# Fourteen pairs of fields instead of twelve, two of their sums on VectorE, other first loads, and dense rows on four row groups

## The chip, the cores and the metric

The kernel runs on one core of one Trainium2 chip. The metric is the device time of one execution in microseconds (us), lower is better. Its engines are PE (TensorE, matrix products), DVE (VectorE), ACT (ScalarE), POOL (GpSimd) and SP (SyncE, which here only issues DMAs). All data are float32.

## What is computed

```python
# e: 512 samples x 39 fields x 16 numbers, one table row per sample and field
e = stack([tbl_f[ids[:, f]] for f in range(39)], axis=1)
x, prev, logit = e, e, []
for k in range(3):                       # three "cross" layers, 128 units each
    z = einsum('bmd,bhd->bdmh', x, prev).reshape(b, D, m * h)
    t = transpose(einsum('bdc,co->bdo', z, ws[k]) + bs[k], (0, 2, 1))
    t = t / sqrt(sum(t * t, axis=(-2, -1), keepdims=True))
    logit.append(t); prev = t
z = sum(concatenate(logit, axis=1), axis=-1)            # 512 x 384
h = maximum(concatenate([z, dense_ctx], axis=1) @ W_top1 + b_top1, 0)   # dense_ctx: 512 x 16
h = maximum(h @ W_top2 + b_top2, 0)
y = h @ W_top3
```

## The kernel before

**Tiles.** The 512 samples go in 16 tiles of 32. A tile's columns are sample and embedding index, N = 32 x 16 = 512, split in two halves N1 and N2 of 256. POOL gathers the table rows by ten indirect DMAs for each tile (`gather`), SP writes them to DRAM as `xt` (one row of 512 numbers for each field) and reads them back spread over partitions.

**Layers 1 and 2** are called k = 1 and k = 2; both have 128 x 39 products in each column. DVE multiplies the previous layer's output (in the PSUM bank `t_ps`) by one field's row on all partitions (`xb`) and writes the product to a ring `z` of 14 slots; PE multiplies `z` by that field's 128 x 128 weights. The 39 fields go in 11 chunks for each layer; "chunk (k, c)" below is chunk c of layer k. `PLAIN_IN` writes the order out: a number n is a plain chunk of n fields (`direct`, two matmuls of 512 columns for each field, one for the left and one for the right 64 weight columns), a 0 is a pair chunk (`pairs`): four fields as two pairs, each pair by a scheme of seven block products instead of eight, so 14 matmuls of 256 columns for a pair chunk. A pair chunk needs sums of its products, which POOL makes (`pair_sums`): first t2 (128 x 512), then t4 and t1 together (128 x 1024, "t41" here). PE starts a pair chunk with eight matmuls on `z` alone, then two on t2, then four on t41. `sums` has two slots, so POOL can be at most two pair chunks ahead of PE; `RING_AT` places chunks in the ring, so that DVE can be two or three ahead.

**Between layers**, `carry` (ACT) and `shared_sums`, `add_shared` (DVE) put the shared parts of the pair scheme together once the last pair chunk is done, and PE may not begin the next layer's first pair chunk before that. PE does layer 0 of the next tile (`layer0`, 14 matmuls of 512 columns) between layer 1 and layer 2 of a tile; DVE prepares it (`products0`) with `xr`, 19 shifted copies of the fields, times `x3`, which ACT first copies to PSUM (`copy_x`). Every engine works through its own list in the written order; semaphores order them.

**Gathers.** POOL issues the ten gathers of tile i + 2 during tile i: five behind the last pair chunk (1, 9) of layer 1, five behind (2, 9). `mix_rows` (POOL) makes combined rows for the pairs behind the first pair chunk.

**The start** gathers tile 0, writes it, loads `xr` and `x3` for tile 0, then all `xb` chunks, then the weights w2, then the rows of tile 1; ACT's list for tile 0 begins with `copy_x(1)`. **The end** is three dense layers; the first has four output blocks of 128, each from three blocks of features and, by a matmul of its own (L794), the 16 dense inputs.

Of the kernel before, what the change touches and what calls it, by code (L numbers as in the profile page):

```python
# [50 lines left out]
PAIR_GROUPS = 3  # L51
PAIRED = 2 * GROUP * PAIR_GROUPS
PAIRS = PAIRED // 2
PLAIN_IN = [3, 3, 0, 0, 3, 0, 0, 3, 0, 0, 3]


def chunks():

    out, field, p = [], PAIRED, 0
    for n in PLAIN_IN:  # L60
        out.append(("D", field, n) if n else ("P", p, 4))
        field, p = field + n, p + (not n)
    return out
# [32 lines left out]


def pair_fields(p):  # L100

    q, j = p // 2, 2 * (p % 2)
    return [(2 * GROUP * q + j + r, 2 * GROUP * q + GROUP + j + r) for r in range(2)]


def build(nc, ids_in, base_in, masks_in, table, xt, xq, dense_t, w0a, w0b, w1, w2, b0, b1, b2,
          wt1, bt1, wt2, bt2, wt3, out):
    ctx = ExitStack()
# [755 lines left out]
```

## Time and profile before

| | |
|---|---|
| Median of the runs shown | 1181.57 us |
| Lowest of them | 1180.67 us |
| The profiled execution's own time | 1181.07 us |
| Its span, first to last instruction | 1179.2 us |
| PE busy | 1124.8 us, 95% |
| DVE busy | 972.1 us, 82% |
| POOL busy | 868.3 us, 74% |
| ACT busy | 126.4 us, 11% |

One of the three runs took 4874.38 us; the median leaves it aside. The profile gives each engine's busy time over the span of one execution. Each float32 matmul of the program is two instructions in it. A busy share near 100% says that an engine is the bound only where no other row shows it waiting, so the trace is read tile by tile.

### The profile page before, as it was taken

The page shows a single profiled execution, that of the slowest core. Times are in us where ns is not written, and L with a number is a line of the kernel's source. Part 1 is how long each engine was busy: PE and PEld are TensorE (multiplying, and loading weights), DVE is VectorE, ACT ScalarE, POOL GpSimd, SP SyncE. Part 2 cuts the span into 40 slices and gives each one's busy share as a digit, 9 for nine tenths or more (in the row PEclk, how much of TensorE's full clock was granted, in tenths as well). Part 3 has the DMA queues.
Part 4 walks back from the last instruction along what each step waited for, and adds up shares of the span by engine and source line. Part 5 has one row for each costly group of instructions (what it writes and reads, how often), then busy time and mean ns, then how long its engine had stood idle before and what let it go on. Part 6 is the DMA issues. An engine that isn't in the chain of part 4 may idle for free. (4 is left out here: it accounts for less than half of the span.)

```text
span 1179.2 us, 21810 instructions
## 1 busy us (share of the span) xinstructions
PE 1124.8 (95%) x7868; PEld 568.1 (48%) x7868; DVE 972.1 (82%) x836; ACT 126.4 (11%) x266; POOL 868.3 (74%) x614
## 2 busy tenths in 40 slices
PE   0789999999999999999999999999999999999999
PEld 0344445455444545544454554545455454545553
DVE  1678889889898988988898898989889898988782
ACT  0000110101011010101101011110101011010102
POOL 5567768788786878877686886868788786856670
PEclk9889999999999999999999999999999999999999
DMA  5958446382744638274463837546382845637010
GB/s 163 382 150 277 142 165 211 98 294 68 286 131 162 210 96 299 68 280 136 144 220 97 306 68 263 154 167 208 95 296 68 282 134 176 211 104 274 1 47 1
DMA packets 104409, 204.31 MB, mean 173 GB/s; under 512 B 49131, under 2 KB 52075, under 8 KB 104390
## 3 DMA queue, kind: packets, MB, share of 16 engines
q1 hardware_dynamic: 97610, 202.52, 51.9%
q0 software_dynamic: 5120, 1.29, 1.1%
q10 hardware_dynamic: 1660, 0.25, 0.2%
q8 instruction: 12, 0.20, 0.1%
q14 instruction: 7, 0.06, 0.0%
HBM read 201.72 MB, written 2.30 MB: 173 GB/s over the span
## 5 line engine op out<-in xcount | busy, mean ns | idle before, releaser
L560 DVE TENSOR_TENSOR z<-t_ps,xb 128x2048 f32<-128x2048 f32 (+1 forms) x352 | 708.1, 2042 | 97.6 <-PE acc L711 73.8
L281 POOL TENSOR_TENSOR sums<-z,sums 128x1024 f32<-128x1024 f32 x192 | 455.4, 2372 | 15.1
L697 PE MATMUL acc<-z,w_sb 128*64 128x512 f32 x1920 | 436.5, 598 | 12.5 <-DVE z L560 12.5
L278 POOL TENSOR_TENSOR sums<-z 128x512 f32<-128x512 f32 x192 | 245.2, 1277 | 193.0 <-DVE z L560 189.2
L711 PE MATMUL mix_ps<-sums,s_sb 128*64 128x256 f32 x1536 | 282.6, 380 | 6.0 <-POOL sums L281 6.0
L697 PEld LDWEIGHTS acc<-z,w_sb 128*64 128x64 f32 x1920 | 137.8, 138 | 246.8 <-issue 224.8
L711 PE MATMUL acc<-z,w_sb 128*64 128x256 f32 x768 | 228.4, 379 | 0.0
L711 PE MATMUL mix_ps<-z,w_sb 128*64 128x256 f32 x768 | 228.4, 379 | 0.0
L711 PE MATMUL acc<-z,s_sb 128*64 128x256 f32 x768 | 228.4, 379 | 0.0
L711 PE MATMUL p_ps<-z,w_sb 128*64 128x256 f32 x768 | 228.4, 379 | 0.0
L711 PEld LDWEIGHTS mix_ps<-sums,s_sb 128*64 128x64 f32 x1536 | 158.8, 137 | 93.6 <-POOL sums L281 13.1
L243 POOL DMA_INDIRECT gathered<-in_table,rows_of x160 | 155.4, 971 | 64.2 <-issue 49.2
L711 PE MATMUL acc<-sums,w_sb 128*64 128x256 f32 x768 | 198.0, 380 | 0.0
L711 PEld LDWEIGHTS acc<-z,w_sb 128*64 128x64 f32 x768 | 105.3, 137 | 97.1 <-issue 55.5
L711 PEld LDWEIGHTS acc<-z,s_sb 128*64 128x64 f32 x768 | 105.2, 137 | 55.4
L688 PE MATMUL acc<-xr,w_sb 117*64 117x512 f32 (+1 forms) x448 | 100.7, 601 | 30.9 <-issue 30.9
L711 PEld LDWEIGHTS mix_ps<-z,w_sb 128*64 128x64 f32 x768 | 105.3, 137 | 0.0
L711 PEld LDWEIGHTS p_ps<-z,w_sb 128*64 128x64 f32 x768 | 105.2, 137 | 0.0
L711 PEld LDWEIGHTS acc<-sums,w_sb 128*64 128x64 f32 x768 | 103.6, 137 | 0.0
L688 PEld LDWEIGHTS acc<-xr,w_sb 117*64 117x64 f32 (+1 forms) x448 | 32.6, 139 | 95.6 <-issue 95.0
L543 DVE TENSOR_TENSOR xr<-t_ps,xr 117x1024 f32<-117x1024 f32 (+1 forms) x60 | 62.3, 1079 | 0.0
L448 ACT COPY cross<-mix_ps 64x256 f32<-64x256 f32 x32 | 11.6, 364 | 376.7 <-PE acc L711 351.1
(76 smaller groups left out, 404.9 us busy)
## 6 DMA issues: line engine op xcount, KB each, us to landing
xb<-xt SPq DMA_DIRECT2D x80, 768.0 KB, 6.8
xb<-xq SPq DMA_DIRECT2D x96, 512.0 KB, 4.7
xb<-xt SPq DMA_DIRECT2D x96, 512.0 KB, 6.3
xr<-xt SPq DMA_DIRECT2D x144, 156.0 KB
x<-xt SPq DMA_DIRECT2D x45, 78.0 KB
gathered<-in_table,rows_of POOLq DMA_INDIRECT x160
xr<-xt SPq DMA_DIRECT2D x32, 78.0 KB
xt<-gathered SPq DMA_DIRECT2D x16, 72.0 KB, 2.3
```

Of the source, the lines that this page charges most:

```text
L243: nc.gpsimd.indirect_dma_start(gathered[0:n, g, :], None, table[:, :], bass.IndirectOffsetOnAxis(rows_of[0:n, g:g + 1], 0)).then_inc(rows_ ...
L278: nc.gpsimd.tensor_tensor(t2, t3, b11, ALU.add).then_inc(sums_ready, 1)
L281: nc.gpsimd.tensor_tensor(t41, b2, t2_twice, ALU.subtract).then_inc(sums_ready, 1)
L448: nc.scalar.copy(cross[RIGHT, N2], mix_ps[LEFT, N2]).then_inc(cross_ready, 1)
L543: nc.vector.tensor_tensor(xr[0:n, k0:k1, :], x[0:n, :].rearrange("p (a n) -> p a n", a=1).broadcast_to([n, k1 - k0, N]), xr[0:n, k0:k1, :] ...
L560: nc.vector.tensor_tensor(z[:, at:at + n, :], t_ps[k - 1][:, :].rearrange("p (a n) -> p a n", a=1).broadcast_to([P, n, N]), xb[:, XB_ROW[c ...
L688: last = nc.tensor.matmul(acc0[o, :], w0_sb[0:n, k, o], xr[0:n, k, :], start=(k == 0), stop=(k == STEPS0 - 1))
L697: last = nc.tensor.matmul(acc[k][o, :], w_sb[k][:, field + r, o], z[:, at + r, :], start=(c == 0 and r == 0), stop=(c == NCH - 1 and r == ...
L711: return nc.tensor.matmul(bank[side, cols], weights, moving, start=start, stop=stop, skip_group_check=True)
```

## The change

- `PAIRS` goes from 12 to 14: seven pair chunks for each layer instead of six, eleven plain fields instead of fifteen, and `PLAIN_IN` is [2, 0, 3, 0, 0, 0, 0, 3, 0, 0, 3] with another `RING_AT`.
- For chunks (1, 5) and (1, 9) t2 is made by DVE (`later_t2`) right behind the chunk's product, from a copy of one operand that ACT makes in PSUM (`copy_b11`, behind `copy_x` in ACT's list). POOL makes the other twelve t2 of a tile and all fourteen t41.
- The gathers are split eight and two instead of five and five; the last gather has its own semaphore, and rows are written before it has landed.
- Layer 0's shifts are grouped so that one DMA on 117 partitions loads what three on 39 did (`load_shifted`, `load_x`); for tile 0, ACT's queue issues some of them. The masks are smaller and loaded apart from the ids.
- DVE's small steps are at other chunks; the mixing of the w2 weights in tile 0 is spread over four chunks; for tile 0 and the last tile the sum of squares comes first.
- The 16 dense inputs are loaded four times, at partitions 0, 32, 64 and 96, and the four matmuls for them each use one such group of 32 rows, one behind the other.

```diff
-PAIR_GROUPS = 3
-PAIRED = 2 * GROUP * PAIR_GROUPS
-PAIRS = PAIRED // 2
-PLAIN_IN = [3, 3, 0, 0, 3, 0, 0, 3, 0, 0, 3]
+PAIRS = 14
+PAIR_GROUPS = -(-PAIRS // GROUP)
+PLAIN_IN = [2, 0, 3, 0, 0, 0, 0, 3, 0, 0, 3]
...
+T2_LATER = {(1, 5): 0, (1, 9): 0}
...
-RING_AT = [0, 3, 6, 10, 0, 3, 7, 11, 0, 4, 8, 11, 0, 3, 7, 11, 0, 4, 8, 0, 4, 10]
+RING_AT = [0, 2, 6, 9, 0, 4, 8, 0, 3, 7, 0, 0, 2, 6, 9, 0, 4, 8, 0, 3, 7, 11]
...
-                pool.wait_ge(rows_gathered, 16 * GROUPS * (i + 1))
-                if not at_first(i):
+                pool.wait_ge(rows_gathered, 16 * (GROUPS - 1) * (i + 1))
...
-                            gather(i + 2, range(0, 5))
+                            gather(i + 2, range(0, 8))
                         if k == 2 and c == LAST_P and gathers:
-                            gather(i + 2, range(5, GROUPS))
-                        if k == 2 and c == FIRST_P + 1 and last:
+                            gather(i + 2, range(8, GROUPS))
+                        if k == 2 and c == PADS_AT and last:
...
+            load_x(act, 0)
+            load_shifted(act, 0, 1)
+            load_shifted(act, 0, 3)
...
+            def copy_b11(i, k):
+                for c in range(NCH):
+                    if (k, c) in T2_LATER:
+                        act.wait_ge(z_ready, chunks_to(i, k, c))
...
+                        nc.scalar.copy(b11_ps[k].rearrange("p (r n) -> p r n", r=2), z[:, at:at + 2, N1]
+                                       ).then_inc(b11_copied, 1)
...
                     copy_x(i + 1)
+                copy_b11(i, 1)
                 carry(i, 1)
...
+            def later_t2(i, k, c):
...
+                        wait_slot(dve, i, k, cc)
+                        dve.wait_ge(b11_copied, t2_count(i, k, cc))
+                        nc.vector.tensor_tensor(sums[:, slot, 0, :, :], z[:, at:at + 2, N2],
+                                                b11_ps[k].rearrange("p (r n) -> p r n", r=2),
+                                                ALU.add).then_inc(vector_t2, 1)
...
                     products(i, 1, c)
-                    if c == 2 and not first:
+                    later_t2(i, 1, c)
+                    if c == 1 and not first:
                         shared_sums(i - 1, 2)
-                    if c == 5 and not first:
+                    if c == 3 and not first:
                         add_shared(i - 1, 2)
-                    if c == 6 and not first:
+                    if c == 7 and not first:
                         norm_sums(2, i - 1)
-                    if c == 6 and first:
-                        mixed_weights(2)
+                    if c >= NCH - 4 and first:
+                        mixed_weights(2, c - NCH + 4)
...
-                    if c == 10:
+                    if c == 8:
                         normalize(i + 1, *layers_of(first, last))
...
-                nc.tensor.matmul(h1_ps[j][:, :], wt1d_sb[:, o], dense_sb[:, :], start=False, stop=False)
+
+            for j in range(TOP1 // P):
+                r = slice(j * DENSE_AT, (j + 1) * DENSE_AT)
+                nc.tensor.matmul(h1_ps[j][:, :], wt1d_sb[r, :], dense_sb[r, :], start=False, stop=False)
```

How it moves instructions, at three places. **POOL, where a tile of the loop goes from layer 1 to layer 2**, before: the two sums of chunk (1, 9), five gathers, the sums of the first pair chunk of layer 2.

```order
L278 TENSOR_TENSOR sums<-z 128x512 [waits z_used,z_ready]
L279 ISA
L281 TENSOR_TENSOR sums<-z,sums 128x1024 [waits sums_ready]
L235 REGISTER_ALU
L237 ISA [waits mixed_ready,xt_written]
L237 TENSOR_TENSOR rows_of<-ids_sb,base_sb 128x10
L239 REGISTER_ALU
L243 DMA gathered<-in_table,rows_of 128x16 [waits rows_ready]
L243 DMA gathered<-in_table,rows_of 128x16 x4
L269 REGISTER_ALU
L278 TENSOR_TENSOR sums<-z 128x512 [waits z_used,z_ready]
```

The same place in the changed kernel (the line numbers are its own):

```order
L335 REGISTER_ALU [waits z_used]
L341 TENSOR_TENSOR sums<-z,sums 128x1024 [waits vector_t2]
L293 REGISTER_ALU
L295 ISA [waits mixed_ready,xt_written]
L295 TENSOR_TENSOR rows_of<-ids_sb,base_sb 128x10
L297 REGISTER_ALU
L301 DMA gathered<-in_table,rows_of 128x16 [waits rows_ready]
L301 DMA gathered<-in_table,rows_of 128x16 x7
L337 REGISTER_ALU [waits z_used]
L338 TENSOR_TENSOR sums<-z 128x512 [waits z_ready]
```

POOL now waits for DVE's t2 at (1, 9), and eight gathers instead of five stand ahead of layer 2's first sums.

**ACT in tile 0**, before: the evacuation of layer 0, a root, the copy of x3 for tile 1, and then the steps behind layer 1.

```order
L431 ACTIVATE sq<-acc,bias 128x512 [waits acc0_ready]
L432 ACTIVATE traw<-acc,bias 128x512
L473 ACTIVATE nrm_ps<-nrm_ps 128x32 [waits nrm_ready]
L439 COPY t_ps<-x 117x512 [waits z_ready,x3_loaded]
L448 COPY cross<-mix_ps 64x256 [waits z_used]
```

And in the changed kernel:

```order
L492 ACTIVATE sq<-acc,bias 128x512 [waits acc0_ready]
L493 ACTIVATE traw<-acc,bias 128x512
L550 ACTIVATE nrm_ps<-nrm_ps 128x32 [waits nrm_ready]
L504 COPY t_ps<-x 117x512 [waits feat_ready,x3_loaded]
L515 COPY acc<-z 128x512 [waits z_ready]
L515 COPY acc<-z 128x512 [waits vector_t2,z_ready]
L525 COPY cross<-mix_ps 64x256 [waits z_used]
```

The two copies for DVE's sums stand behind the copy of x3 for tile 1, which waits for that load.

**DVE in tile 0**, in the changed kernel, from the product of chunk (1, 2) on:

```order
L643 TENSOR_TENSOR z<-t_ps,xb 128x1536
L643 TENSOR_TENSOR z<-t_ps,xb 128x2048 x3
L656 TENSOR_TENSOR sums<-z,acc 128x512
L643 TENSOR_TENSOR z<-t_ps,xb 128x2048
L643 TENSOR_TENSOR z<-t_ps,xb 128x1536
L612 TENSOR_TENSOR s_sb<-w_sb 128x768
L612 TENSOR_TENSOR s_sb<-w_sb 128x128
```

The first sum L656 stands between the products of chunks (1, 5) and (1, 6); before, the products of the two chunks followed each other.

## Rows read from the trace of the kernel before

**Rows 1.** The page: busy us (share of the span) and instructions by engine.
```profile
PE 1124.8 (95%) x7868; PEld 568.1 (48%) x7868; DVE 972.1 (82%) x836; ACT 126.4 (11%) x266; POOL 868.3 (74%) x614
```

**Rows 2.** Windows of two whole tiles: us, busy us (instructions) by engine, PEclk, DMA, GB/s.
```profile
226.11:294.37 68.26, 68.26 (x490) 34.57 (x488) 60.06 (x52) 7.54 (x16) 53.84 (x39) 1.00 0.55 180
294.37:364.52 70.15, 68.63 (x490) 34.74 (x488) 60.15 (x52) 7.53 (x16) 53.98 (x39) 1.00 0.53 175
```

**Rows 3.** Timeline of PE in the first of them: start, us, what.
```profile
226.11 6.18 PE L688 MATMUL acc<-xr,w_sb 117*64 117x512 f32 x28
232.12 5.32 PE L697 MATMUL acc<-z,w_sb 128*64 128x512 f32 x24
...
239.00 0.81 PE L711 MATMUL mix_ps<-sums,s_sb 128*64 128x256 f32 x5
...
242.02 0.81 PE L711 MATMUL mix_ps<-sums,s_sb 128*64 128x256 f32 x5
...
247.62 0.81 PE L711 MATMUL mix_ps<-sums,s_sb 128*64 128x256 f32 x5
```

**Rows 4.** Groups by line and shape: count, busy us, mean ns, idle before.
```profile
L281 POOL TENSOR_TENSOR sums<-z,sums 128x1024 f32<-128x1024 f32 x192 | 455.4, 2372 | 15.1
L560 DVE TENSOR_TENSOR z<-t_ps,xb 128x2048 f32<-128x2048 f32 x192 | 437.5, 2286 | 74.1 <-PE acc L711 73.8
...
L278 POOL TENSOR_TENSOR sums<-z 128x512 f32<-128x512 f32 x192 | 245.2, 1277 | 193.0 <-DVE z L560 189.2 <-issue 3.7
...
L243 POOL DMA_INDIRECT gathered<-in_table,rows_of x160 | 155.4, 971 | 64.2 <-issue 49.2 <-POOL rows_of L237 13.1
...
L591 DVE TENSOR_TENSOR acc<-acc,v 128x512 f32<-128x512 f32 x16 | 11.0, 690 | 0.1
```

**Rows 5.** Timelines at one change of layer: POOL's last sum, ACT's first copy.
```profile
565.43 2.37 POOL L281 TENSOR_TENSOR sums<-z,sums 128x1024 f32<-128x1024 f32 x1
```
```profile
569.79 0.36 ACT L448 COPY cross<-mix_ps 64x256 f32<-64x256 f32 x1 [16.28 <-PE acc L711]
```

**Rows 6.** Timelines: two gathers with a gap, and a wait of PE.
```profile
332.04 0.94 POOL L243 DMA_INDIRECT gathered<-in_table,rows_of  x1 [2.49 <-issue]
```
```profile
343.80 0.43 PE L711 MATMUL mix_ps<-sums,s_sb 128*64 128x256 f32 x1 [1.28 <-POOL sums L281]
```
```profile
917.10 0.94 POOL L243 DMA_INDIRECT gathered<-in_table,rows_of  x1 [2.24 <-issue]
```

**Rows 7.** Timelines of the start: SP, DVE and PE.
```profile
23.59 3.84 SPq L343 DMA_DIRECT2D xr<-xt  x9
```
```profile
34.78 1.82 DVE L543 TENSOR_TENSOR xr<-x,xr 117x1024 f32<-117x1024 f32 x2 [1.79 <-DMA xr<-xt]
```
```profile
30.92 8.01 PE L688 MATMUL acc<-xr,w_sb 117*64 117x512 f32 x28 [30.92 <-issue]
```

**Rows 8.** Windows of the start, in the columns of Rows 2.
```profile
30.00:32.50 2.50, 1.58 (x4) 0.59 (x6) 1.51 (x2) 0.00 (x0) 2.20 (x2) 1.00 1.07 209
...
35.00:40.00 5.00, 3.93 (x20) 1.08 (x16) 1.60 (x2) 1.03 (x2) 3.38 (x4) 1.00 1.02 409
```

**Rows 9.** Timelines of tile 0: SP, ACT, PE, and PE's start of tile 1's layer 0.
```profile
69.73 1.16 SPq L338 DMA_DIRECT2D x<-xt  x3
```
```profile
72.62 0.59 ACT L439 COPY t_ps<-x 117x512 f32<-117x512 f32 x1 [30.29 <-DMA x<-xt]
```
```profile
73.76 5.34 PE L697 MATMUL acc<-z,w_sb 128*64 128x512 f32 x12 [4.84 <-DVE z L560]
...
87.55 6.18 PE L688 MATMUL acc<-xr,w_sb 117*64 117x512 f32 x28
```

**Rows 10.** Timeline of PE in the last tile and behind it.
```profile
1121.73 5.37 PE L697 MATMUL acc<-z,w_sb 128*64 128x512 f32 x24 [3.53 <-DVE z L560]
...
1155.74 1.02 PE L794 MATMUL acc<-xb 128*128 128x512 f32 x2
1156.60 1.88 PE L792 MATMUL acc<-feat,xb 128*128 128x512 f32 x4
```

More of the change, by code:

```diff
@@ L32, with pair_fields @@
 STEPS0 = -(-SHIFTS // PER_STEP)
-SHIFT_OF = [[PER_STEP * k + j + 1 for j in range(PER_STEP)] for k in range(STEPS0 - 1)] + [[SHIFTS - 1, 0]]
+SHIFT_OF = [[k + STEPS0 * j for j in range(PER_STEP) if k + STEPS0 * j < SHIFTS] for k in range(STEPS0)]
 WIDE = PER_STEP * FIELDS
-NARROW = 2 * FIELDS
+NARROW = len(SHIFT_OF[-1]) * FIELDS
 XT_ROWS = FIELDS + SHIFTS - 1
 LOADS0 = [(0, 2), (2, 4), (4, 6), (6, 7)]
-PAIR_GROUPS = 3
-PAIRED = 2 * GROUP * PAIR_GROUPS
-PAIRS = PAIRED // 2
-PLAIN_IN = [3, 3, 0, 0, 3, 0, 0, 3, 0, 0, 3]
+PAIRS = 14
+PAIR_GROUPS = -(-PAIRS // GROUP)
+PLAIN_IN = [2, 0, 3, 0, 0, 0, 0, 3, 0, 0, 3]
+def pair_fields(p):
+    q, j = p // 2, 2 * (p % 2)
+    return [(2 * GROUP * q + j + r, 2 * GROUP * q + GROUP + j + r) for r in range(2)]
 def chunks():
-    out, field, p = [], PAIRED, 0
+    out, p = [], 0
+    paired = [m for p in range(PAIRS // 2) for ab in pair_fields(p) for m in ab]
+    plain = [m for m in range(FIELDS) if m not in paired]
     for n in PLAIN_IN:
-        out.append(("D", field, n) if n else ("P", p, 4))
-        field, p = field + n, p + (not n)
+        out.append(("D", plain[0], n) if n else ("P", p, 4))
+        plain, p = plain[n:], p + (not n)
     return out
@@ L68, with chunk_of @@
 XB_ROW = [sum(n for _, _, n in CHUNKS[:c]) for c in range(NCH + 1)]
+def chunk_of(row):
+    return next(c for c in range(NCH) if XB_ROW[c + 1] > row)
+PADS_AT = next(c for c in range(chunk_of(4), NCH) if CHUNKS[c][0] == "P")
 FIRST_P = PLAIN_IN.index(0)
@@ L72 @@
 STEPS = 2 * NCH
+PAIR_CHUNKS = [(k, c) for k in (1, 2) for c in range(NCH) if CHUNKS[c][0] == "P"]
+T2_LATER = {(1, 5): 0, (1, 9): 0}
+VECTOR_T2 = [kc for kc in PAIR_CHUNKS if kc in T2_LATER]
+POOL_T2 = [kc for kc in PAIR_CHUNKS if kc not in T2_LATER]
 RING = 14
-RING_AT = [0, 3, 6, 10, 0, 3, 7, 11, 0, 4, 8, 11, 0, 3, 7, 11, 0, 4, 8, 0, 4, 10]
+RING_AT = [0, 2, 6, 9, 0, 4, 8, 0, 3, 7, 0, 0, 2, 6, 9, 0, 4, 8, 0, 3, 7, 11]
 def ring_back(s):
@@ L90 @@
 SUM_SLOTS = 2
+QUADS = [q for q in ((0, PAIRS // GROUP, GROUP), (PAIRS // GROUP, 1, PAIRS % GROUP)) if q[2]]
 LEFT, RIGHT = slice(0, UNITS // 2), slice(UNITS // 2, UNITS)
@@ L97 @@
 DENSE = 16
-def pair_fields(p):
-    q, j = p // 2, 2 * (p % 2)
-    return [(2 * GROUP * q + j + r, 2 * GROUP * q + GROUP + j + r) for r in range(2)]
+DENSE_AT = 32
 def build(nc, ids_in, base_in, masks_in, table, xt, xq, dense_t, w0a, w0b, w1, w2, b0, b1, b2,
@@ L121, in build @@
         rows_of = sb("rows_of", [P, GROUPS], I32)
-        masks = sb("masks", [P, 2, PAIR_GROUPS, EMB])
+        masks = sb("masks", [P, 2])
         gathered = sb("gathered", [P, GROUPS, EMB])
@@ L657, in _ @@
             dve.wait_ge(w0b_loaded, 16)
[L659 to L663 removed]
+            nc.vector.tensor_tensor(w0_sb[:, :, :], w0_sb[:, :, :], w0m, ALU.add).then_inc(w0_ready, 1)
+            for part in range(4):
+                mixed_weights(1, part)
             products0(0, range(len(LOADS0)))
[L665 to L666 removed]
+            sum_squares(0, 0)
+            sum_d(0, 0, dsum_alone)
+            normalize(0, 0, 1, dsum_alone)
             scale0(0)
@@ L765, in tile @@
                     layer0(i + 1)
-                layer(i, 2, range(0, 7), first)
+                layer(i, 2, range(0, 6), first)
                 add_partitions(i + 1, *layers_of(first, last))
-                layer(i, 2, range(7, NCH), first)
-            pe.wait_ge(w0_ready, 2)
+                layer(i, 2, range(6, NCH), first)
+            pe.wait_ge(w0_ready, 1)
             pe.wait_ge(ones_ready, 1)
```

226 lines of the change are left out of this document (134 added, 92 removed).

## The prediction

> **What bounds the kernel now.** I read the page's busy shares first, then single tiles. PE is busy for 95% of the span, DVE for 82%, POOL for 74% [rows 1]. The windows of two whole tiles say how firm that is: in one of 68.26 us PE is busy for all 68.26, while DVE has 60.1 and POOL 53.8 of busy time [rows 2]. So in a plain tile PE is the bound and nothing waits. The next window is 70.15 us long, and 1.5 us of it is PE idle: POOL was late. The engine behind PE is POOL, though its busy share hides that: its gathers cost more than their busy time. The group has 971 ns for each of 160 gathers and 49.2 us of "issue" before them [rows 4], so about 1.25 us each with the usual gap of 0.3. A tile costs POOL 12 x (1.28 + 2.37) + 10 x 1.25 + some 2 for row numbers and mixing, that is 58 of 68 us. And buffers are short: `sums` holds two pair chunks, so POOL's spare time can't be saved up.
>
> PE's prices come from its timeline [rows 3]: the same point of two pair chunks in a row is 3.02 us apart (239.00 and 242.02); the next is 5.60 later, with three plain fields between, so a plain field is 2.58 / 3 = 0.86; layer 0 is 6.01 (226.11 to 232.12).
>
> **1. The extra pair chunk.** In each layer four plain fields (3.44) become a pair chunk (3.02): -0.42. Of 32 layers, the first is counted in step 3; 31 x 0.42 = **-13.0 us**. This lies on PE, the bound, and it is real only where PE stays fed.
>
> **2. Feeding PE in a plain tile.** POOL now has 14 x 2.37 + 12 x 1.28 + 12.5 + 2 = 63 us of 67.4: two t41 more. DVE gets two 128x512 sums at 0.69 [rows 4], each behind an ACT copy of about 0.6, so 60.1 + 1.4 busy and 1.3 of waiting: 63 too. Neither is over PE's 67.4, so the question is the places where work meets. I walked the new order with these durations; the tight place is the change from layer 1 to 2. Let PE end chunk (1, 5) at 0. DVE's product (1, 8) is there at 2.4, one part of `xr` at 3.5, product (1, 9) at 5.7; ACT's copy ends at 6.5, DVE's t2 at 7.3, POOL's t41 at 9.7. PE needs it 2.2 into (1, 9), at 10.8: 1.1 to spare, near the lead that POOL has now (its sum ends at 567.80, PE's chunk at about 569.7, its last four matmuls take 0.9) [rows 5]. Then POOL does row numbers and eight gathers: 0.2 + 0.8 + 1.0 + 7 x 1.25 = 10.8, to 20.5; then t2 and t41 of (2, 1), to 24.2. PE meanwhile: end of (1, 9) 11.6, of (1, 10) 14.2, of layer 0 20.2, two fields to 22.0, and t41 wanted at 24.1. Before, POOL had 6.8 us of gathers and PE six fields instead of two between the same points: 3.4 + 4 less room now. So the spare time is zero, 0.1 short. The run of four pair chunks (2, 3) to (2, 6) also eats 0.65 of lead for each chunk (3.67 on POOL against 3.02); at (2, 6) the two meet within 0.1, at (2, 9), behind DVE's scaling steps that moved to c = 8, POOL is 0.1 late. Sum of the walk 0.2 us a tile, 14 tiles of the loop: **+2.8 us**. Bounds: 0, where my walk is 0.3 pessimistic at each place, and 1.0 a tile, 14 us, where it is 0.3 optimistic at each of three places. I take the walk itself. The new early wait of PE at FIRST_P = 1 for the shared sums costs nothing: ACT's and DVE's steps take some 3.3 us (an estimate: two copies and five small sums) from the end of (2, 9), PE has 2.6 + 1.7 of work.
>
> **3. Start and tile 0.** ACT's copy for DVE's t2 of (1, 5) stands behind `copy_x(1)`, and that waited for its load until 72.62 [rows 9]. Before, nobody needed it early; PE had a wait of 4.84 there anyway, for w2 at DVE. Now DVE, and everything behind it on DVE's list (products (1, 6) on, the w2 weights), stands still until the load lands, with PE stopped inside (1, 5), which it would reach near 56 to 58. When does it land? The loads start about 2.0 earlier than 23.59 [rows 7] (masks apart, rows written before the last gather). The first loads move slowly, 209 GB/s with the DMA engines full, against 409 later [rows 8]; they are 2 KB pieces on 39 partitions and become 4 KB pieces on 117. At the later rate that would give up to 4 more; I take 1.8. So the load lands near 68.8, ACT's two copies end at 70.1, DVE's t2 at 70.8. From there, at 0: POOL t41 2.4, PE ends (1, 5) 3.2; DVE (1, 6) 2.2, POOL 6.1, PE ends (1, 6) 7.0 and (1, 7) 9.6, (1, 8) 12.6; DVE (1, 9) 11.9 after the weights' first parts, t2 13.3, POOL 15.7, PE ends (1, 9) 16.6; DVE's (1, 10) 17.4, PE 20.0. PE's layer 0 of tile 1 starts at 90.8 instead of 87.55: **+3.2 us**, though the very first matmuls come some 5 us earlier. The bounds are the load's: 66.6 to 72.6, that is +1 to +7. PE's clock is at half behind the stop (twelve instructions took 5.34 at 73.76 [rows 9], three fields take 2.58 elsewhere [rows 3]), but there PE waits for POOL most of the time; I leave it in the range. One short wait more at tile 0's (2, 1), where DVE is late as well: **+0.6**.
>
> **4. The gathers' gaps.** At about every 29th gather of the run POOL stops: 2.49 us at 332.04, 2.24 at 917.10, two others like them [rows 6]. A gap in the second batch cost PE its length less 0.6 (70.15 - 68.26 = 1.9 for 2.49 [rows 2]; one of its two waits is in [rows 6]); the one at 917.10 fell in the first batch, where the room was wide, and cost nothing. With eight gathers in the first batch the 58th, 87th and 145th all fall there, and there is no room now: 2 x 0.6 + 2.2 = **+3.4 us**. Bounds 0 and +8 (a fourth gap).
>
> **5. The last tile's change of layer**, without a layer 0 as cover. PE waited 3.53 [rows 10]. The first product is shorter by 0.5, but behind it PE has two fields instead of six: it waits 0.5 for the product of (2, 1), then 1.6 for t41, and 0.9 in the run of four: 6.0 instead of 4.0, **+2.1 us**.
>
> **6. The dense rows.** Four matmuls of 0.86 (1155.74 to 1156.60) at the end, on the path. Two instructions each, so 0.43 for one [rows 10]. No row shows row groups. The nearest are the left and right column halves: there 24 instructions of the same 512 columns take 5.3, 0.22 each [rows 3], so two halves overlap fully. I take it that four on four row groups take one's time: **-2.6 us**, bound 0. The matmuls left between the norm's one and its use are five, 4.3 us, more than the chain of small operations beside them (some 2, an estimate from their short forms).
> The Trainium skill ("TensorEngine Tiling (Array Packing)", Key Properties) has two rules here that pull apart: tiles "can execute LdWeights and Matmul in parallel", and changing the tiling mode "drains the TensorE". By the first the sum stays as it is; by the second alone the gain is smaller. No row here tells the price of a drain.
>
> **Sum.** -13.0 + 2.8 + 3.2 + 0.6 + 3.4 + 2.1 - 2.6 = -3.5. The span of 1179.2 becomes 1175.7; the profiled execution's own time is 1.9 above its span, and the median 0.5 above that: **1178 us**.
>
> **Rivals.**
> A. *PE stays fed.* Steps 2 and 4 cost nothing and the load of step 3 lands early: -13.0 - 2.6 + 1.0 + 2.1 = -12.5, 1169 us; with tile 0 better by 4 still, 1165. For it: POOL and DVE are below PE in every total. Against: totals of 63 against 67 with two slots of buffer. Chance 0.27.
> B. *POOL becomes the bound*, slower than before. Place: eight gathers ahead of (2, 1). If a gather costs 0.1 more in a batch of eight (at the start, in batches of ten, several took longer), or DVE's t2 comes 1 us later, PE waits 1 us in each tile, and each gap counts in full: -3.5 + 11 + 4 = +11.5, 1193 us. It beats the gain from about 0.45 us a tile on. Chance 0.2.
> C. *The row groups do not overlap:* the -2.6 is gone, 1181 us. The skill's rule on mode changes would do this. Chance 0.08, as the column halves speak for overlap.
>
> **How the numbers follow.** My forecast, 1178, has 0.45. The range of 8 in 10 runs from the middle of A to B: 1164 to 1192. A measurement of this kernel tells about 2% from no change; faster by that means under 1158, which needs all of A and 7 us more: 0.04. Slower by it, over 1205, needs B at twice its price: 0.02. Within 2%: 0.94.
>
> **What would show it.** Plain tiles: layer 0 to layer 0 near 67.6; PE waits on POOL's sums in (2, 1) up to 0.4, and of 2 to 3 us in about three tiles, with a gap among the eight gathers. Tile 0: ACT's copy of x3 ends near 69.5, DVE's first L656 right behind, PE stopped over 10 us before it. PE's layer 0 of tile 1 starts near 91. The four dense matmuls within 1 us. I am wrong if waits of PE are in other places (the shared sums, DVE's products), or if the load for tile 1 comes before 60.

## The result, and the profile after

The changed kernel takes **1254.43 us** (median of four runs, 1252.67 to 1258.84) against 1181.12 for the kernel before on the same chip: a ratio of 1.063 with a 95% interval of 1.059 to 1.067. It is slower by 6%, where I had forecast 1178 us and a range up to 1192. The span of the profiled execution is 1257.0 us, against 1179.2.

The page of the changed kernel, busy time by engine (before: [rows 1]):
```profile
PE 1131.8 (90%) x8252; PEld 589.7 (47%) x8252; DVE 995.2 (79%) x875; ACT 144.3 (11%) x298; POOL 946.6 (75%) x646
```
PE has only 7 us more of busy time, so 71 of the 78 us more of span are waiting. Where, is told by PE's starts of layer 0, in tile 1 and in tile 15 (timeline of PE in the changed kernel):
```profile
127.62 5.66 PE L798 MATMUL acc<-xr,w_sb 117*64 117x512 f32 x24
...
1125.36 6.18 PE L798 MATMUL acc<-xr,w_sb 117*64 117x512 f32 x28
```
Before, tile 1's came at 87.55 [rows 9] and tile 15's at 1049.85 (timeline of PE in the kernel before):
```profile
1049.85 6.18 PE L688 MATMUL acc<-xr,w_sb 117*64 117x512 f32 x28
```
So the start and tile 0 lose 40.1 us, the 14 tiles between lose 997.7 - 962.3 = 35.4 (71.3 us a tile), and the rest 2.3. Both losses have one name, in the view of waits of the changed kernel (waited for: us in total, times, longest):
```profile
ACT t_ps L504 <- DMA x<-xt: 79.6, 15, 29.1
DVE xr L626 <- DMA xr<-xt: 75.3, 30, 12.8
...
PE acc L798 <- DVE xr L626: 55.6, 3, 41.7
...
PE mix_ps L821 <- POOL sums L341: 26.0, 23, 2.1
PE acc L807 <- DVE z L643: 25.7, 17, 3.7
```
ACT and DVE wait for the loads of x3 and `xr`. PE itself never waits for a DMA, it waits for POOL's sums and DVE's products, which stand behind those two on their engines' lists. In a plain tile (SP, ACT and DVE timelines of the changed kernel, 671 to 700):
```profile
671.55 0.79 SPq L272 DMA_DIRECT2D x<-xt  x1
672.45 10.28 SPq L279 DMA_DIRECT2D xr<-xt  x4
...
677.65 0.59 ACT L504 COPY t_ps<-x 117x512 f32<-117x512 f32 x1 [3.26 <-DMA x<-xt]
...
678.79 0.69 DVE L656 TENSOR_TENSOR sums<-z,acc 128x512 f32<-128x512 f32 x1 [1.37 <-ACT acc L515]
...
696.19 1.22 DVE L626 TENSOR_TENSOR xr<-t_ps,xr 117x1024 f32<-117x1024 f32 x1 [1.92 <-DMA xr<-xt]
699.40 0.69 DVE L626 TENSOR_TENSOR xr<-t_ps,xr 78x512 f32<-78x512 f32 x1 [1.99 <-DMA xr<-xt]
```
x3 is issued at 671.55 and is there at 677.65; the last part of `xr` lands at 699.40, 28 us behind the first issue. How the DMA engines spend that time is in the windows of the changed kernel (last columns: PEclk, DMA share, GB/s):
```profile
672.00:677.50 5.50, 5.50 (x43) 2.79 (x40) 5.38 (x4) 1.34 (x2) 5.34 (x4) 1.00 0.19 55
...
683.00:690.00 7.00, 7.00 (x56) 3.79 (x54) 7.00 (x6) 0.00 (x0) 5.67 (x4) 1.00 0.19 77
```
and in a window of the kernel before, over the loads of the same data:
```profile
552.00:556.00 4.00, 4.00 (x28) 1.85 (x26) 3.58 (x4) 1.48 (x3) 3.92 (x3) 1.00 0.81 216
```
The share of the 16 DMA engines stands at 0.19, which is 3 of 16, for 25 us; before it is 0.81, which is 13 of 16. The merged source counts 3 shifts in its outermost dimension and 39 fields in the next; before, each DMA's outermost dimension counted 39, and 13 is its largest divisor up to 16.

The Trainium skill ("DMA: Bandwidth & Descriptors", section "Why a DMA increments its semaphore by 16 and not by 1", at "How many engines (k)") states this: the slowest dimension of size over 1 of source and destination decides, and the largest k up to 16 that divides both is the number of engines. By it 3 and 117 give 3, 39 and 39 give 13; the trace agrees with 0.19 and 0.81. I had not drawn on it. The same page of the Trainium skill ("Rules for kernel authors") also has that "an outermost dim of size c < 16 [...] confines the whole DMA to at most c engines".

Tile 0 pays first for its own loads. Timelines of PE and ACT at the start of the changed kernel, where PE stops inside layer 0 each time until the next part of `xr` has landed and been multiplied by DVE:
```profile
41.69 3.68 PE L798 MATMUL acc<-xr,w_sb 117*64 117x512 f32 x8 [41.69 <-DVE xr L626]
55.59 5.83 PE L798 MATMUL acc<-xr,w_sb 117*64 117x512 f32 x16 [10.21 <-DVE xr L626]
65.10 1.97 PE L798 MATMUL acc<-xr,w_sb 78*64 78x512 f32 x4 [3.67 <-DVE xr L626]
...
67.12 0.69 ACT L492 ACTIVATE sq<-acc,bias 128x512 f32<-128x512 f32 x1 [63.45 <-PE acc L798]
```
Before, PE did this layer in one go from 30.92 on, 8.01 us long [rows 7]; so 28 us are lost before layer 1 of tile 0 begins. The wait for tile 1's x3 is then no longer than before: ACT waits 29.07 us for it, where it waited 30.29, until 72.62 [rows 9]. It only comes later, and DVE now stands behind it (SP, ACT and DVE in the changed kernel):
```profile
91.92 0.76 SPq L272 DMA_DIRECT2D x<-xt  x1
...
98.30 0.59 ACT L504 COPY t_ps<-x 117x512 f32<-117x512 f32 x1 [29.07 <-DMA x<-xt]
98.83 0.58 ACT L515 COPY acc<-z 128x512 f32<-128x512 f32 x1
...
99.51 0.69 DVE L656 TENSOR_TENSOR sums<-z,acc 128x512 f32<-128x512 f32 x1 [14.73 <-ACT acc L515]
```
A whole tile of the changed kernel in one window, to be held against [rows 2]:
```profile
626.64:697.91 71.27, 68.32 (x515) 36.20 (x513) 61.06 (x53) 8.65 (x18) 58.98 (x41) 1.00 0.52 173
```
PE is idle for 3 us in each tile, two waits of over 1 us, for DVE's product and for POOL's sum (PE's timeline of the changed kernel):
```profile
634.08 1.94 PE L807 MATMUL acc<-z,w_sb 128*64 128x512 f32 x8 [1.26 <-DVE z L643]
...
640.08 0.43 PE L821 MATMUL mix_ps<-sums,s_sb 128*64 128x256 f32 x1 [1.42 <-POOL sums L341]
```
Two things are better than before. The longest gap ahead of a gather is 0.3 us, where [rows 6] have 2.49 and 2.24 (waits of POOL in the changed kernel):
```profile
POOL gathered L301 <- issue: 40.3, 135, 0.3
```
And the four dense rows run beside each other: those in the last rows of PE's timeline start within 0.55 us, where before each took 0.86 [rows 10], 3.4 for the four:
```profile
1241.38 0.70 PE L906 MATMUL acc<-xb 32*128 32x512 f32 x2
...
1241.91 0.59 PE L906 MATMUL acc<-xb 32*128 32x512 f32 x2
```

### The profile page after: what moved, and what is told of

Same layout as the page of the kernel before. It is cut to its first block and busy times, and to the rows that moved or that the text cites. A ratio compares the mean times of both kernels' runs of the same rounds, so it can differ in the third digit from the quotient of the medians.

```text
span 1257.0 us, 22412 instructions
## 1 busy us (share of the span) xinstructions
PE 1131.8 (90%) x8252; PEld 589.7 (47%) x8252; DVE 995.2 (79%) x875; ACT 144.3 (11%) x298; POOL 946.6 (75%) x646
## 5 line engine op out<-in xcount | busy, mean ns | idle before, releaser
L643 DVE TENSOR_TENSOR z<-t_ps,xb 128x2048 f32<-128x2048 f32 (+2 forms) x352 | 705.1, 2040 | 49.4 <-PE acc L821 37.3
L341 POOL TENSOR_TENSOR sums<-z,sums 128x1024 f32<-128x1024 f32 x224 | 533.0, 2380 | 56.2 <-DVE sums L656 41.2
L821 PE MATMUL mix_ps<-sums,s_sb 128*64 128x256 f32 x1792 | 338.5, 382 | 36.5 <-POOL sums L341 26.0
L807 PE MATMUL acc<-z,w_sb 128*64 128x512 f32 x1408 | 328.2, 603 | 25.7 <-DVE z L643 25.7
L821 PE MATMUL acc<-z,w_sb 128*64 128x256 f32 x896 | 268.7, 382 | 3.6 <-DVE z L643 3.6
L821 PE MATMUL mix_ps<-z,w_sb 128*64 128x256 f32 x896 | 268.6, 382 | 0.0
L821 PE MATMUL acc<-z,s_sb 128*64 128x256 f32 x896 | 267.4, 380 | 0.0
L821 PE MATMUL p_ps<-z,w_sb 128*64 128x256 f32 x896 | 267.4, 380 | 0.0
L821 PEld LDWEIGHTS mix_ps<-sums,s_sb 128*64 128x64 f32 x1792 | 182.3, 137 | 150.7 <-POOL sums L341 52.0
L821 PE MATMUL acc<-sums,w_sb 128*64 128x256 f32 x896 | 233.8, 383 | 0.0
L656 DVE TENSOR_TENSOR sums<-z,acc 128x512 f32<-128x512 f32 x32 | 22.0, 688 | 51.2 <-ACT acc L515 50.5
```

Source lines behind the costliest of these rows:

```text
L341: nc.gpsimd.tensor_tensor(t41, b2, t2_twice, ALU.subtract).then_inc(t41_ready, 1)
L643: nc.vector.tensor_tensor(z[:, at:at + n, :], t_ps[k - 1][:, :].rearrange("p (a n) -> p a n", a=1).broadcast_to([P, n, N]), xb[:, XB_ROW[c ...
L656: nc.vector.tensor_tensor(sums[:, slot, 0, :, :], z[:, at:at + 2, N2], b11_ps[k].rearrange("p (r n) -> p r n", r=2), ALU.add).then_inc(vec ...
L807: last = nc.tensor.matmul(acc[k][o, :], w_sb[k][:, field + r, o], z[:, at + r, :], start=(c == 0 and r == 0), stop=(c == NCH - 1 and r == ...
L821: return nc.tensor.matmul(bank[side, cols], weights, moving, start=start, stop=stop, skip_group_check=True)
```

## The experiments

Theory 1: the merged loads' outermost dimension confines them to 3 engines, and x3 and `xr` land late; all else is near my forecast. Rivals: 2, the rest of the change costs it (pairs, gathers, PE badly fed); 3, ACT's list alone, where the copies for DVE's sums stand behind x3's. "Split" below means loads on 39 partitions. Ratios are to the kernel before, in runs on the same chip.

**1. Split loads in the changed kernel.**
```diff
-            src = bass.AP(blk.tensor, blk.offset, [[0, PER_STEP], [N, FIELDS], [1, N]])
-            engine.dma_start(x3[:, :], src).then_inc(x3_loaded, 16)
+            for j in range(PER_STEP):
+                engine.dma_start(x3[j * FIELDS:(j + 1) * FIELDS, :], blk[0:FIELDS, :]).then_inc(x3_loaded, 16)
```
and the same for `xr`, one DMA for each shift.

> The changed kernel with each merged load of x3 and xr taken apart again: three DMAs (two for the last step) on 39 partitions each, with the new shifts and 4 KB pieces. Nothing else differs. Theory 1 (the merged loads run on 3 of the 16 DMA engines, because their outermost dimension is 3: the DMA share was 0.19 = 3/16 while they ran alone): they get the speed of before, tile 0 loses its 28 us of late loads, the plain tiles their waits behind layer 0 (71.3 to about 67.7 us a tile), and the time falls to 1178 us, the sum of the prediction, 1165 to 1192. Theory 2 (the seventh pair chunk, the sums on VectorE and the new order are themselves too tight, the late loads only a symptom): the time stays over 1230 us.

Measured: 1182.9 us, ratio 1.0005 (0.9994 to 1.0017), span 1181.0. 76 of the 78 us are gone: 24.1 up to layer 0 of tile 1, 48.1 in the 14 tiles, 3.8 behind them. A tile takes (1053.13 - 103.54) / 14 = 67.83 us, and in one PE is idle for 0.08 (window of the kernel with split loads):
```profile
578.20:646.00 67.80, 67.72 (x514) 36.44 (x512) 60.93 (x54) 8.72 (x18) 58.76 (x40) 1.00 0.56 181
```
Theory 1 holds, rival 2 falls as the cause of the 6%. Tile 0 stays bad: layer 0 of tile 1 starts at 103.54, 16 us later than before. Timelines of SP, ACT, DVE and POOL there, in the same kernel:
```profile
46.88 22.87 SPq L383 DMA_DIRECT2D xt<-gathered  x4
...
71.72 1.15 SPq L272 DMA_DIRECT2D x<-xt  x3
...
74.49 0.59 ACT L505 COPY t_ps<-x 117x512 f32<-117x512 f32 x1 [31.09 <-DMA x<-xt]
...
75.70 0.69 DVE L657 TENSOR_TENSOR sums<-z,acc 128x512 f32<-128x512 f32 x1 [16.35 <-ACT acc L516]
...
80.17 3.30 DVE L613 TENSOR_TENSOR s_sb<-w_sb 128x768 f32<-128x768 f32 x2
...
80.20 3.12 POOL L342 TENSOR_TENSOR sums<-z,sums 128x1024 f32<-128x1024 f32 x1
```
DVE stands still for 16.35 us behind ACT's copy, which waits for x3 as I had written, but x3 lands at 74.5 and not at 68.8. Its load is issued no earlier than before (71.72 against 69.73 [rows 9]): SP is busy for 22.87 us issuing the four writes of tile 1's rows that stand ahead of it, so the earlier start did not reach this load.

**2. The kernel before with merged loads**, nothing else changed (its shifts are grouped as in the change).

> The kernel before with the merged loads alone (shifts k, k + 7, k + 14 in one DMA on 117 partitions; x3 in one DMA; tile 0 as well, on the queues of before). Theory 1: tile 0's layer 0 is late by some 25 to 30 us, and tile by tile the last part of xr lands 20 to 22 us after the first is issued, some 3 us after DVE wants it: 1220 to 1250 us. Theory 2: within 1% of the kernel before, 1170 to 1193.

Measured: 1304.58 us, ratio 1.102 (1.099 to 1.105). The merged loads alone cost 10% in the old kernel, more than in the new and more than either theory's number; the cause is the same (its view of waits):
```profile
DVE xr L540 <- DMA xr<-xt: 105.0, 46, 9.8
PE acc L691 <- DVE z L557: 71.1, 18, 4.6
```
One part of the higher cost is that PE runs slower here. Page, PE's timeline in one tile, and the window behind the stop, in this kernel:
```profile
PE 1167.8 (90%) x7868; PEld 571.8 (44%) x7868; DVE 977.4 (75%) x835; ACT 126.5 (10%) x266; POOL 865.2 (66%) x614
```
```profile
650.73 8.24 PE L691 MATMUL acc<-z,w_sb 128*64 128x512 f32 x24 [4.00 <-DVE z L557]
```
```profile
650.00:656.00 6.00, 5.28 (x14) 1.58 (x16) 6.00 (x4) 0.64 (x2) 1.31 (x2) 0.50 0.69 253
```
PE stops for 4.00 us in one piece, and behind it the granted clock is 0.50 of full speed; the 24 matmul instructions take 8.24 us instead of 5.32 [rows 3]. So 43 of the 124 us of added span are PE busy for longer over the same 7868 instructions (1167.8 against 1124.8 [rows 1]). In the changed kernel the stops in a tile are 1.26 and 1.42, and its clock over the tile is 1.00. Why the stop is longer in the old kernel was not tested; its rows are written behind five gathers of the second batch instead of two, so the same slow load starts later.

**3 and 4. The two t2 of DVE back on POOL**, with merged and with split loads.
```diff
-T2_LATER = {(1, 5): 0, (1, 9): 0}
+T2_LATER = {}
```

> The changed kernel with all fourteen t2 on GpSimd and no copies in PSUM, merged loads kept. Theory 1: xr still lands late, so the time stays within 15 us of the changed kernel, 1240 to 1270 us. Theory 3 (the late load of x3 acts only through ACT's list, where the copy for VectorE's sum stands behind it): tile 0 and the plain tiles recover most of the loss, under 1215.

> Both edits: loads taken apart and all t2 on GpSimd. Beside e1_split it prices the two sums on VectorE. If GpSimd is as near its limit as the prediction had it (63 of 67.4 us a tile), 2.6 us more a tile make it wait-bound: 10 to 20 us slower than e1_split in the plain tiles, less some 8 us in tile 0, where nothing stands behind x3's copy: 0 to +12 us in all. If VectorE's list is the tight one, it is faster than e1_split by 5 us or more.

Measured: merged 1251.57 us, ratio 1.058 (1.056 to 1.060), a tile still 71.5; split 1180.93, ratio 0.9992 (0.998 to 1.0003). Rival 3 falls as the whole cause: without any copy behind x3's the loss is nearly whole, through DVE's products of layer 0. (That ACT's list can carry a part of it is shown by experiment 10.) The split pair shows what DVE's sums are worth: with them on POOL a tile takes 68.58 us, 0.75 more, but layer 0 of tile 1 starts at 90.04, 13.5 us sooner. Gain in the loop and loss in tile 0 nearly cancel.

**5. ACT's copy for chunk (1, 5) ahead of x3's copy, in tile 0 only**, split loads.
```diff
+                if first:
+                    copy_b11(i, 1, range(0, 7))
                 if not last:
                     copy_x(i + 1)
-                copy_b11(i, 1)
+                copy_b11(i, 1, range(7 if first else 0, NCH))
```

> e1_split with one step moved in tile 0: ACT's copy for the sum of chunk (1, 5) ahead of its copy of x3 for tile 1. Theory: in e1_split PE stood 11.7 us in tile 0 for that sum alone. With it gone, tile 1's layer 0 starts near 90 us, as in e4_split_poolt2 (90.0), instead of 103.5, while the plain tiles keep 67.85: 1169 us. Rival: VectorE runs into the w2 weights and the x3 of tile 1 right behind, and gives most of it back: over 1177.

Measured: 1173.41 us, ratio 0.993 (0.991 to 0.995); layer 0 of tile 1 starts at 92.50 instead of 103.54. So 11 of the 16 us lost in tile 0 were that one place in ACT's list. The gain is less than the 2% at which I count a kernel as changed, but its interval lies below 1, as do those of experiments 9, 11 and 13.

**6. Tile 1's rows, x3 and `xr` ahead of the weights w2 on SP**, on top of 5.
```diff
-            sp.dma_start(w_sb[2][:, :, :], w2.rearrange("(m h) o -> h m o", h=P)).then_inc(w_loaded[2], 16)
             write_rows(1)
...
             load_layer0(1)
+            sp.dma_start(w_sb[2][:, :, :], w2.rearrange("(m h) o -> h m o", h=P)).then_inc(w_loaded[2], 16)
```

> e5_b11_first with SP's order in tile 0 changed: the rows, x3 and xr of tile 1 ahead of the load of w2, which needs less in front of it than they do. Expected: x3 for tile 1 is there some 8 us sooner, w2 some 8 later, in time for the mixing of its weights only if that does not stand in the way of the products: 1161 to 1171 us. Rival: VectorE, which mixes the w2 weights from chunk (1, 7) on, now waits longer for w2 and stops everything: over 1173.

Measured: 1182.95 us, ratio 1.0006 (0.9996 to 1.0016). The entry's rival holds: x3 comes sooner, and the wait moves to w2 (DVE's timeline, and PE's wait):
```profile
83.33 1.16 DVE L615 TENSOR_TENSOR s_sb<-w_sb 128x768 f32<-128x768 f32 x2 [18.57 <-DMA w_sb<-in_w]
```
```profile
PE acc L824 <- DVE z L646: 15.2, 1, 15.2
```

**7. The 39 rows written as 3 x 13**, split loads of experiment 1: the pattern begins [[13 * N, 3], [N, 13], ...].

> e1_split with its DMAs on 39 partitions written with the 39 rows as 3 x 13, so that the outermost dimension of the source is 3 instead of 39: same bytes, same pieces, same count of DMAs and issues. Theory 1 (the outermost dimension sets how many DMA engines work): the loads run on 3 of 16 engines again, DMA share 0.19 while they are alone, and the time is back at 1235 to 1270 us. Rival (the size of one DMA, or its 117 partitions, made it slow): within 1% of e1_split, 1171 to 1194.

Measured: 1182.81 us, ratio 1.0009 (0.9999 to 1.0019), as with 39: no slow load. 13 rows of 512 follow the 13 before without a break, so the two dimensions are one run of 39, and it may be that they were joined before the DMA was made. It doesn't test the rule; experiment 9 does.

**8. Gathers five and five**, split loads of experiment 1.

> e1_split with the ten gathers split five and five again. By the prediction's walk eight ahead of chunk (2, 1) leave no room and cost 0 to 0.4 us a tile, so this would gain up to 5 us, if the three more behind (2, 9) find room; if they don't, PE waits in the next tile's first pair chunks for 1 to 2 us a tile: 1177 to 1210 us. If the place of the gathers does not matter, within 3 us of e1_split.

Measured: 1230.55 us, ratio 1.042 (1.039 to 1.045), 3.2 us a tile more on the mean and 4.0 in half of the tiles, which is outside both expectations. Timelines of ACT and PE in one tile:
```profile
648.22 0.59 ACT L505 COPY t_ps<-x 117x512 f32<-117x512 f32 x1 [4.05 <-DMA x<-xt]
```
```profile
640.98 0.65 PE L822 MATMUL mix_ps<-sums,s_sb 128*64 128x256 f32 x4 [0.28 <-POOL sums L339]
643.40 0.59 PE L822 MATMUL mix_ps<-sums,s_sb 128*64 128x256 f32 x1 [1.77 <-POOL sums L342]
```
Five gathers behind (2, 9) end at 639.6, then come the sums of (1, 1), for which PE is waiting; and the rows of the next tile are written only then, so x3 is 4 us late for ACT. My walk had found no room ahead of (2, 1); the tight place is this one, and eight and two is what serves it.

**9. One DMA on 117 partitions again, with the field outermost**, on top of 5. Partition 3 x field + shift instead of 39 x shift + field; the layer 0 weights are laid out to match.
```diff
-            src = bass.AP(blk.tensor, blk.offset + k0 * N, [[STEPS0 * N, shifts], [N, FIELDS], [1, (k1 - k0) * N]])
+            src = bass.AP(blk.tensor, blk.offset + k0 * N, [[N, FIELDS], [STEPS0 * N, PER_STEP], [1, (k1 - k0) * N]])
```

> Kernel: the one with split loads and the early copy for chunk (1, 5) (1173.4 us, span 1171.6), but the loads are again one DMA each on 117 partitions, as in the changed kernel, with the other order of partitions: field outermost, shift inside (partition = 3 x field + shift). So the source's outermost dimension counts 39 instead of 3, and rows, bytes and number of DMAs are those of the changed kernel. The last step is loaded for three shifts, the third against weights of zero. Theory 1, the outermost dimension counts out the DMA engines: the DMA share during these loads is 0.8 or so, not 0.19; layer 0 to layer 0 stays at 67.8 us; 1170 to 1176 us. Theory 2, the merged DMA itself is slow (117 partitions, or 468 KB in one piece): the share stays at 0.19, 71.3 us a tile, 1230 us or more.

Measured: **1171.4 us** (1170.36 to 1171.89, five runs), ratio 0.991 (0.990 to 0.993). Window of its load, and PE's starts of layer 0 in tiles 1 and 15:
```profile
612.00:614.00 2.00, 2.00 (x22) 1.33 (x20) 2.00 (x2) 0.59 (x1) 1.92 (x3) 1.00 0.76 258
```
```profile
91.13 4.46 PE L798 MATMUL acc<-xr,w_sb 117*64 117x512 f32 x19
...
1042.05 6.18 PE L798 MATMUL acc<-xr,w_sb 117*64 117x512 f32 x28
```
Partitions, pieces and number of DMAs are the changed kernel's (its last step has one shift more); only the order of the two dimensions differs, and the share goes from 0.19 to 0.76. So it is not that a merged DMA is slow. The merging was sound, its outermost dimension was not.

**10. Only x3 merged with 3 outermost**, on top of 5.

> Kernel: the same one of 1173.4 us, but only x3 is loaded by one DMA with an outermost dimension of 3; xr stays on 39 partitions. It sizes the slow load where it is short: 234 KB at the 75 GB/s of the merged loads take 3.1 us instead of under 1. ACT's copy of x3 then waits 2 to 3 us instead of 0.2 in a plain tile. If only lateness at DVE counts (theory 1), most of this is hidden, since the first product of layer 0 comes 3 to 4 us later: 67.8 to 68.5 us a tile and up to 2 us more in tile 0, 1174 to 1185 us. If a slow load holds up the loads behind it on the same queue (theory 3), the parts of xr land late too and a tile is near 71: 1215 us or more.

Measured: 1205.75 us, ratio 1.022 (1.019 to 1.024), 69.9 us a tile. Window and ACT's timeline:
```profile
628.50:632.00 3.50, 3.50 (x24) 1.50 (x22) 3.46 (x4) 1.34 (x2) 3.05 (x2) 1.00 0.38 78
```
```profile
635.98 0.59 ACT L505 COPY t_ps<-x 117x512 f32<-117x512 f32 x1 [4.49 <-DMA x<-xt]
```
Between the expectations: ACT waits 4.5 us for x3, not 2 to 3, and 2 us reach PE in each tile. The path is ACT's list and not theory 3 of that entry (loads held up behind x3): from tile 2 on no product of `xr` waits for a load, while DVE's sums wait for the copy behind x3's (DVE's timeline):
```profile
637.12 0.69 DVE L659 TENSOR_TENSOR sums<-z,acc 128x512 f32<-128x512 f32 x1 [2.61 <-ACT acc L516]
```
So the slow loads hurt on two paths, late `xr` at DVE (experiment 3) and late x3 through ACT's copy (this one). From issue to copy x3 takes 7.4 us here and 3.2 in kernel 1; why it is more than the expected 2 to 3 apart, these runs don't settle.

**11 and 12. The last gather's semaphore**, which I looked at because the gaps of [rows 6] were gone. 11 is the kernel before with it, 12 is kernel 9 without it.
```diff
-                        bass.IndirectOffsetOnAxis(rows_of[0:n, g:g + 1], 0)).then_inc(rows_gathered, 16)
+                        bass.IndirectOffsetOnAxis(rows_of[0:n, g:g + 1], 0)
+                        ).then_inc(rows_gathered if g < GROUPS - 1 else last_gathered, 16)
...
-                pool.wait_ge(rows_gathered, 16 * GROUPS * (i + 1))
+                pool.wait_ge(rows_gathered, 16 * (GROUPS - 1) * (i + 1))
```

> Kernel: before, with one thing of the change: the last gather of each tile counts on a semaphore of its own, and the mixing of rows and the first write wait for nine gathers instead of ten. It is about the gaps: before's gathers 29, 58, 87 and 145 are each preceded by 2.2 to 3.3 us of idle POOL, while the changed kernel has none, even with its gathers five and five. Theory S, they hang on all ten gathers counting on one semaphore: the gaps are gone (longest 0.3 us), and the time falls by the two that cost PE something, 2 to 4 us of 1181. Rival, they come from something else in the changed program (where its buffers and its code lie, its masks): the four gaps stay at the same gathers, and the time is within 1 us of before's.

> Kernel: the one with the field as outermost dimension (1171.4 us, span 1169.9), with that one thing undone: all ten gathers count on one semaphore, and mixing and writing wait for all ten. Theory S: gaps of 2 to 3 us before gathers 29, 58, 87 and 145 are back; eight gathers stand ahead of chunk (2, 1), where there is little room, so up to 1.5 to 2.5 us each for three of them, 3 to 8 us in all: 1174 to 1180 us. Rival, something else: no gap over 0.3 us, 1171 to 1173 us (rows written some 0.5 us later at the start).

Measured: 11 takes 1173.0 us, ratio 0.992 (0.990 to 0.994); 12 takes 1185.14, ratio 1.004 (1.002 to 1.005). POOL's waits in 11, and POOL's timeline in 12 at its 145th gather:
```profile
POOL gathered L243 <- issue: 39.9, 132, 0.3
```
```profile
916.66 0.95 POOL L299 DMA_INDIRECT gathered<-in_table,rows_of  x1 [0.30 <-issue]
919.90 0.94 POOL L299 DMA_INDIRECT gathered<-in_table,rows_of  x1 [2.29 <-issue]
```
The gaps go with the semaphore in both directions, by 8 and by 14 us, more than the 2 to 4 and 3 to 8 that I had expected. In 11 layer 0 of tile 1 starts at 84.26, 3.3 sooner, and the loop's period is 68.26, 0.48 less: exactly the plain tile of [rows 2]. In 12 the loop takes 965.7 us against 950.9; its four gaps (3.7, 3.2, 2.2 and 2.3) are 11.4 of those 14.8, and the other 3.4 stay open. Where the gather whose turn it is stands first of its batch (the 116th before, the 29th in 12), POOL shows no gap.

**13 and 14. What of it.** 13 is kernel 9, where mixing and writing wait for both semaphores; 14 is kernel 12 with 128 rows in the last gather too.
```diff
 pool.wait_ge(rows_gathered, 16 * (GROUPS - 1) * (i + 1))
+pool.wait_ge(last_gathered, 16 * (i + 1))
+pool.sem_inc(all_gathered, 1)
```
```diff
-                    n = P if g < GROUPS - 1 else LAST_GROUP * TILE_B
+                    n = P
```

> Kernel: the one with the field as outermost dimension (1171.4 us). The last gather keeps its own semaphore, but now mixing waits for all ten gathers (both semaphores), and POOL then tells SP, which writes all rows behind that. Theory S1, the gaps hang on which semaphore the gathers count on: no gap over 0.3 us, gathers' issue idle 35 to 40 us in all. Theory S2, they hang on waiting for all ten: four gaps of 2 to 3 us at gathers near 29, 58, 87, 116 and 145. The time is no measure here, as rows are written about 1 us later in each tile, and x3 lands that much later: 1172 to 1186 us by S1, 1182 to 1195 us by S2.

> Kernel: the one with all ten gathers on one semaphore (1185.1 us, gaps at gathers 58, 87, 116 and 145), but the last gather of a tile takes 128 rows like the others, not 96; the 32 more are never read. Theory S1 or S2 alone: the gaps stay, at other gathers if they follow the number of rows issued (29 gathers are 3648 rows, so every 28th or 29th), 1184 to 1187 us. Theory U, the gaps need gathers of unequal size on one semaphore: no gap over 0.3 us, 1171 to 1175 us.

Measured: 13 takes 1170.97 us, ratio 0.992 (0.990 to 0.994), no gap over 0.3; 14 takes 1180.11, ratio 0.999 (0.998 to 1.0006), under the 1184 to 1187 expected, with gaps of 3.07, 2.22, 2.16 and 1.58 ahead of gathers 57, 85, 113 and 141. So it is the semaphore and not the wait for ten, and unequal sizes are not needed. The period fits a count of rows: 28 gathers of 128 are 3584 rows, 29 of before are some 3620. Two sizes of the last gather are all that this rests on.

## Why the prediction was wrong, point by point

**The step that failed** is in step 3: "they are 2 KB pieces on 39 partitions and become 4 KB pieces on 117. At the later rate that would give up to 4 more; I take 1.8." I took merging to be neutral or better, put the load's bounds at 66.6 to 72.6, and in the walk of step 2 took the loads of a plain tile as there in time. They run on 3 of 16 DMA engines: PE's layer 0 of tile 0 ends 28 us late, x3 for tile 1 is there at 98.3 instead of 68.8, and in a plain tile the last part of `xr` is multiplied 28 us after the first issue. Price: 76 us of span (experiment 1), more than everything else in the sum. The Trainium skill's rule ("DMA: Bandwidth & Descriptors", as above) would have given it ahead: an estimate by it is 3/16 of the 409 GB/s of [rows 8], 77 GB/s, so 24 us for the 1794 KB of a tile's x3 and `xr`; the windows shown have 55 and 77.

The other steps are read from kernel 1, which is the change without the slow loads (1182.9 us against 1178):
- **Steps 1 and 2**, an extra pair chunk and feeding PE: 67.83 us a tile against "near 67.6". Kernel 11 gives the price without the gaps: 68.26 - 67.83 = 0.43 us a tile gained, where I had 0.84 - 0.2 = 0.64. Right in kind, short by 0.2 a tile.
- **Step 3**, tile 0: the mechanism was right, DVE and PE behind ACT's copy behind x3, but +16.0 instead of +3.8 (with the 0.6 at (2, 1)). x3 lands at 74.5, not 68.8, as its load is issued no earlier than before; and mixing the w2 weights, which moved in between, takes 3.3 us for two instead of 1.2, since POOL works beside it. 11 us of it could have been saved by one copy moved (experiment 5).
- **Step 4**, the gaps: wrong in sign. I read their period and placed them in the batch of eight; I never asked what they hang on, though the diff changes the semaphore that the gathers count on. In the kernel before it gives 6.7 us back in the loop (11), where I had the gaps cost 3.4 more. With all ten gathers on one semaphore the changed order would have lost 14.8 us in the loop (12 against 9), 8.1 more than before, which is the upper bound that I had put.
- **Steps 5 and 6**, with the last pair chunks: -1.5 behind tile 15's layer 0, where my terms give -1.8. The dense rows are right: 1.1 us instead of 3.4 in kernel 1.

Rival A (PE stays fed) is near what the change is worth without its two mistakes: it said 1169, kernels 9 and 13 take 1171. The nearness is luck: A has no gain from a semaphore, and of what 9 gains over before, 10 us, the semaphore makes 8 (kernel 11, 1173.0). Rival C did not happen, and nor did B as written: POOL's late sums make PE wait in the changed kernel, but behind the merged loads, and with split loads PE is idle for 0.08 us in a tile. The rest of the change, with loads and copy mended, gives 4.7 in the loop and 3.3 at the end over kernel 11 and loses 6.9 up to tile 1's layer 0.

In my list of what would show me wrong stood waits "in other places (the shared sums, DVE's products)": that is where they are, at 634.08, for a reason that the list didn't have.

## What to carry to other kernels

Before merging DMAs, count the outermost dimension of source and destination: put the one with many rows there, and read the DMA share in a window over the load, where 0.19 says 3 of 16. A load on few engines costs twice where it stops PE for long: behind a stop of 4 us the clock was at half. Of a load that moves, cost it in the plain tile too, not only where it is first seen late. When a periodic stall is in the profile, ask what resource has that period before placing it; a semaphore of its own for one gather in ten was worth more here (8 us) than the extra pair chunk (0.43 us a tile, 6 in the loop).

## What the runs showed of the hardware

- **Gathers on one semaphore.** With all ten gathers of a tile counting on one semaphore, POOL's issue stops for 1.6 to 3.7 us about every 3600 gathered rows (kernels before, 2, 12, 14); with the last on its own it never does (all other kernels here). Why a second semaphore does this is open; no run shows what POOL waits for in the gap, and none varies the buffer that the program sets for such DMAs (`dynamic_dma_scratch_size=4096`).
- **DVE and POOL beside each other.** Two of DVE's sums with both inputs in SBUF take 3.30 us beside POOL's, 1.2 with POOL idle (83.33 above), and POOL's 2.37 becomes 3.12. The Trainium skill ("GPSIMD Engine Reference", Specifications) names this contention for instructions with two SBUF inputs, without a size.
- **Row groups.** Four products of 32 rows on four row groups take 1.1 us, where four of 128 rows one behind the other took 3.4. A drain at the change of mode, which the Trainium skill ("TensorEngine Tiling (Array Packing)", Key Properties) names, would have to be within that.
- **TensorE's clock.** In experiment 2 the granted clock is 0.50 (1.2 GHz) in the 6 us behind a stop of 4.00 us. Behind the same wait of 2.99 us in the last tile, eight instructions take 3.62 us in the changed kernel, 3.53 in kernel 1 and 1.94 in kernel 9, and the granted clock in the 15 us from there is 0.89, 0.89 and 1.00 (1.2 GHz for a part of the first two, 2.4 throughout the third). Kernel 1 has split loads, so the merged loads do not make this difference; what does is open. The 3.8 us that the end costs more with merged loads lie in the tile before it, where PE waits 1.41 and 1.49 us for products and sums.
